# Graph network kernel: expansion ahead of the gathers, landed rows added by Vector, node numbers fetched 16 steps at a time

## The chip, the cores and the metric

The kernel runs on one core of one Trainium2 chip. The metric is the device time of one execution in microseconds, lower is better. It was measured three times before the change: 10926.67, 10941.0 and 10946.07 us, median 10941.0.

## The reference, cut to what matters

A graph has N = 12500 nodes with 64 channels and E = 200000 edges (`src`, `dst`, 16 attributes each), sorted by `dst`, whose distribution is uneven. Two blocks follow each other, each with a residual and a layer norm around it; each block goes over the edges twice.

```python
# block 1, two times (relu after each)
z = concat([x[dst], x[src]]); m = sigmoid(z @ Wf + bf) * softplus(z @ Ws + bs)
x = x + segment_sum(m, dst)
# block 2, two times (batch norm after each): attention over the edges and a self loop per node
alpha = leaky_relu(a_src[src] + a_dst[dst] + a_edge)
p = exp(alpha - segment_max(alpha)[dst]) / segment_sum(...)
out = segment_sum(xl[src] * p, dst)
```

## The kernel before, in words

Nodes lie in NB = 98 blocks of P = 128. Setup sorts the edges into steps: a step is up to 128 edges, one per partition, which all go to one block of 128 destination nodes. There are STEPS = 1664 steps in 13 batches of 128. Eight steps are a unit (UNIT; 208 units in a stage), and most buffers exist twice (SETS = 2), one for even units and one for odd ones. `dst_rel` holds each edge's node number within its block, and `rel_rows` in HBM the same by step, as bf16, for the transposed use.

The four edge stages are the loops over all steps. The first two (`cg_edges`, block 1) do this per unit. GpSimd issues a gather for each step (L706): 128 rows of 128 floats from `q_table`, the source node's part of z @ W, into `ring`, four groups of four steps. SyncE fetches the unit's node numbers to all 128 partitions (L684), one DMA per unit. Vector compares them with the partition's number and so makes the transposed one-hot (L737). TensorE forms `pre` in PSUM, in two halves of four steps (`form`): it adds the gathered rows by a matmul with the identity (L797), and expands the destination node's part out of `p_tab` with the transposed one-hot (L801). Scalar takes |pre|, Exp and Ln (L766 to L771), Vector finishes both softplus halves (L742, L743), Scalar does one more Exp (L776), Vector multiplies to the message (L749) and makes the one-hot (L587, in `build_onehot`). TensorE sums the messages by node (`segment_sum`, L815, between an opening and a closing matmul, L602 and L609), and Vector adds the eight sums to the accumulator (L728).

The last two stages (`gat_edges`, block 2) gather 65 floats per step (L1166) into two buffers of a whole batch each, expand two numbers per edge with the transposed one-hot (L1187, L1382), do the softmax of a batch while the messages of the batch before it are summed, and then weigh and sum as above (L1289, L587, L1434, L1284). Their node numbers are fetched by L1137, one DMA per unit.

Nothing plans the order; each engine runs its own list, written out by `stages(u, first, last, (lag, what), ...)`: in turn u it does `what` for unit u - lag, in the order of the list. In `cg_edges` Vector's turn is `add(u-3), spread(u-1), onehot_t(u), softs(u-1), message(u-1)`, and TensorE's is the first half of `form(u)`, the second half of the sums of u-2, the second half of `form(u)`, the first half of the sums of u-1. The engines meet at semaphores, and the ones that matter are these. GpSimd may gather into a group's slot when TensorE has formed the half that used it (`s_X0`, `s_X`, L697). TensorE's identity matmul waits for the gathered rows (`s_row`). Scalar and Vector wait for `s_X`; Vector's `add` for the closed sums (`s_agg`); the expansion for the one-hot (`s_T`). SyncE fetches into a slot when Vector has read it; there are four slots of a unit each in `cg_edges` and two in `gat_edges`. In `gat_edges` GpSimd gathers into a buffer's slots unit by unit, when Vector has made the messages of two batches before (`e_m`), and Vector's one-hot waits for the expansion before it (`a_X`).

Of the kernel before, what the change touches and what calls it, by code (L numbers as in the profile page):

```python
# [23 lines left out]
P = 128  # L24
# [626 lines left out]
def cg_edges(k, layer):  # L651
# [4 lines left out]
    (s_zero, s_S, s_T, s_X0, s_X, s_ln, s_softf, s_softs, s_sig, s_msg, s_agg, s_acc, s_idx, s_act) = (  # L656
        k.sem(n + x) for x in ("zero", "onehot", "onehot_t", "pre_half", "pre", "ln", "soft_f", "soft_s", "sig", "msg", "agg", "acc", "idx", "act"))
# [3 lines left out]
    s_rel = [k.sem(f"{n}rel{q}") for q in range(CG_UNROLL)]  # L661
    p_tab = k.big[:, 0:NB * 2 * C]
    ring = k.big[:, NB * 2 * C:NB * 2 * C + RING].rearrange("p (u i c) -> p u i c", u=UNROLL, c=2 * C)
    acc = k.wide[:, NB * C:NB * (C + AW)]
    rel = rel_slots(k.wide[:, 0:CG_UNROLL * GROUP * P], CG_UNROLL)
    at = CG_UNROLL * GROUP * P
    turned = by_set(k.wide[:, at:at + UNROLL * GROUP * P].rearrange("p (u i c) -> p u i c", u=UNROLL, c=P))
    soft = by_set(k.work[:, 0:UNROLL * GROUP * P].rearrange("p (u i c) -> p u i c", u=UNROLL, c=2 * C))
    onehot, msg = by_set(k.onehot), by_set(k.msg)
    pre = [k.pairs[j][:, :, :].rearrange("p u (i c) -> p (u i) c", c=2 * C) for j in range(SETS)]  # L670
# [4 lines left out]
    with nc.Block() as block:  # L675
        @block.sync
        def _(sp):
            k.clear_old(sp)

            def fetch(it):  # L680
                for q in range(CG_UNROLL):
                    wait(sp, s_T, (it - 1) * CG_UNROLL + q + 1 if not isinstance(it, int) or it else 0)
                    sp.sem_inc(s_turn, 1)
                    sp.dma_start(rel[q], rel_row(k, it * CG_UNROLL + q)).then_inc(s_rel[q], 16)  # L684
            fetch(0)
            with sp.Fori(1, CG_ITERS) as it:
# [27 lines left out]
        def _(v):  # L714
# [5 lines left out]
            def iteration(it, first, last):  # L720
                n = counts(v, it * CG_UNROLL, -3, 3)
# [12 lines left out]
                def onehot_t(c):  # L734
                    v.wait_ge(s_rel[c], it * 16 + 16)
                    wait(v, s_X, n[c - 1])
                    nc.vector.tensor_scalar(turned[c % SETS].rearrange("p i c -> p (i c)"), rel[c], k.iota_col[:, :], None, ALU.is_equal).then_inc(s_T, 1)  # L737
# [13 lines left out]
                for u in range(CG_UNROLL):  # L751
                    stages(u, first, last, (3, add), (1, spread), (0, onehot_t), (1, softs), (1, message))
# [30 lines left out]
        def _(pe):  # L783
            def iteration(it, first, last):
                n = counts(pe, it * CG_UNROLL, -2, 4)
                gathered = it * (CG_UNROLL // SETS * 16 * GROUP)
                blocks, slots = {}, {}

                def form(c, half):

                    j, u = c % SETS, 2 * (c % SETS) + half
                    if half == 0:
                        blocks[c] = load_offsets(k, pe, TAB_ROW, it * (CG_UNROLL * UNIT) + c * UNIT, UNIT, (NB - 1) * 2 * C)
                    pe.wait_ge(s_row[u], gathered + (16 * GROUP * (c // SETS + 1) + row_base[u]))
                    if half == 0:
                        wait(pe, s_softs, n[c - 1])
                    nc.tensor.matmul(k.psum[u][:, :], k.ident[:, :], ring[:, u].rearrange("p i c -> p (i c)"), start=True, stop=False)  # L797
# [827 lines left out]
```

## Time and profile before

| | |
|---|---|
| three runs | 10926.67, 10941.0, 10946.07 us |
| the profiled execution's own time | 10924.85 us |
| its span, first to last instruction | 10923.1 us |
| TensorE, GpSimd, Vector, Scalar busy | 56, 62, 35, 17% |
| mean granted TensorE clock | 0.612 of full |
| gathers | 2 x 3328 |
| fetches of node numbers | 832, 256 KB each |

How to read it: the profile is one execution. PE is TensorE's matmul part and PEld its weight loads, DVE is Vector, ACT Scalar, POOL GpSimd, SP SyncE. L12 is line 12 of the kernel above, and a line can be that of a helper. A busy time counts no register, branch or issue work. The end of a matmul is modelled. An fp32 matmul has two records. "Idle before" is the engine's idle time just before the group's instructions, with what ended it: "issue" is that nothing shown was waited for, "remote" that a semaphore was updated at a time at which no instruction shown had just ended.

### The profile page before, as it was taken

How to read it: one execution, taken by the hardware profiler on the slowest of the kernel's cores; microseconds unless marked ns; L12 is line 12 of the kernel's file. 1: busy time of each engine (PE TensorE's matmuls, PEld its weight loads, DVE VectorE, ACT ScalarE, POOL GpSimd, SP SyncE). 2: the span in 40 equal slices, each digit the busy share in tenths (PEclk: the TensorE clock that was granted, in tenths of full speed). 3: DMA queues.
4: the chain of work that ended last, by engine and by line, in shares of the span. 5: the costliest groups of instructions: out<-in, count | busy, mean ns of one | idle time of the engine just before them, and what ended most of it. 6: DMA issues, size and time to landing. Idle time of an engine off the chain costs nothing. (4 is left out here: it accounts for less than half of the span.)

```text
span 10923.1 us, 113136 instructions
## 1 busy us (share of the span) xinstructions
PE 6133.0 (56%) x30283; PEld 4722.4 (43%) x30284; DVE 3780.2 (35%) x5844; ACT 1828.7 (17%) x2603; POOL 6747.6 (62%) x6802
## 2 busy tenths in 40 slices
PE   2777777777777777777413444444471344444446
PEld 1555555555555555555303333333350333333335
DVE  6333333333333333333402323223250222332226
ACT  1333333333333333333200000000010000000000
POOL 2666666666566666666366666666606666666661
PEclk6777777777777777777555555555555555555555
DMA  4222222222222222222322212222112221222221
GB/s 138 65 65 66 67 66 66 67 66 63 77 65 66 65 66 67 66 66 66 69 49 43 45 42 45 44 44 45 39 21 48 44 45 42 43 44 45 43 43 26
DMA packets 436626, 612.01 MB, mean 56 GB/s; under 512 B 180134, under 2 KB 217754, under 8 KB 434779
## 3 DMA queue, kind: packets, MB, share of 16 engines
q0 software_dynamic: 214032, 332.71, 13.7%
q1 hardware_dynamic: 217116, 262.20, 8.3%
q10 hardware_dynamic: 5193, 13.44, 0.4%
q8 instruction: 162, 2.65, 0.1%
q14 instruction: 123, 1.01, 0.0%
HBM read 575.04 MB, written 32.78 MB: 56 GB/s over the span
## 5 line engine op out<-in xcount | busy, mean ns | idle before, releaser
L706 POOL DMA_INDIRECT big<-q_table,idx_stage x3328 | 3309.7, 995 | 1592.7 <-issue 957.9
L1166 POOL DMA_INDIRECT big<-xl_table,idx_stage x3328 | 3336.2, 1002 | 1524.1 <-issue 1018.9
L1434 PE MATMUL bank<-msg,onehot 128*128 128x66 f32 x6656 | 1603.1, 410 | 1025.8 <-issue 974.9
L1434 PEld LDWEIGHTS bank<-msg,onehot 128*128 128x128 f32 x6656 | 1510.3, 325 | 1196.2 <-issue 1194.7
L801 PEld LDWEIGHTS bank<-big,wide 128*128 128x128 f32 x6656 | 1243.0, 263 | 1451.8 <-issue 1450.4
L801 PE MATMUL bank<-big,wide 128*128 x6656 | 1289.8, 351 | 774.3 <-DVE wide L737 495.3
L797 PE MATMUL bank<-big,ident 128*128 128x512 f32 x1664 | 1261.6, 846 | 172.9 <-DMA big<-q_table,idx_stage 93.0
L815 PE MATMUL bank<-msg,onehot 128*128 128x67 f32 (+1 forms) x6656 | 1156.7, 324 | 313.2 <-issue 213.5
L815 PEld LDWEIGHTS bank<-msg,onehot 128*128 128x128 f32 x6656 | 1073.9, 241 | 450.7 <-issue 448.9
L1284 DVE TENSOR_TENSOR wide<-wide,bank 128x528 f32 x416 | 293.0, 704 | 2457.6 <-DMA work<-in_dst 896.8
L587 DVE TENSOR_TENSOR onehot<-iota,dst_rel 128x1024 f32<-128x1024 f32 x832 | 1014.9, 1220 | 0.0
L1382 PE MATMUL bank<-spread_bf,big 128*128 x3328 | 275.6, 172 | 1292.8 <-issue 1166.4
L766 ACT ACTIVATE work<-bank 128x1024 f32<-128x1024 f32 x416 | 424.6, 1021 | 3041.0 <-remote 2502.8
L728 DVE TENSOR_TENSOR wide<-wide,bank 128x536 f32 (+1 forms) x416 | 291.7, 701 | 1724.3 <-remote 1610.3
L1382 PEld LDWEIGHTS bank<-spread_bf,big 128*128 128x128 bf16 x3328 | 200.4, 105 | 1363.0 <-issue 1347.3
L742 DVE SCALAR_TENSOR_TENSOR work<-bank,work 128x512 f32<-128x512 f32 x416 | 287.6, 691 | 1356.8 <-issue 698.9
L602 PE MATMUL bank<-zero_bf 1*128 1x268 bf16 x1664 | 467.6, 365 | 439.2 <-DVE onehot_t L1199 222.3
L1187 DVE TENSOR_SCALAR big<-big,iota_col 128x1024 bf16<-128x1024 bf16 x416 | 207.1, 500 | 1064.3 <-remote 911.0
L771 ACT ACTIVATE work<-work 128x1024 f32<-128x1024 f32 x416 | 439.6, 1057 | 51.6
L768 ACT ACTIVATE work<-work 128x1024 f32<-128x1024 f32 x416 | 439.6, 1057 | 13.3
L797 PEld LDWEIGHTS bank<-big,ident 128*128 128x128 f32 x1664 | 325.1, 241 | 220.8 <-issue 112.0
L1355 ACT ACTIVATE msg<-work 128x16 f32<-128x16 f32 x224 | 48.4, 220 | 2052.8 <-DMA work<-in_dst 648.4
(226 smaller groups left out, 3515.3 us busy)
## 6 DMA issues: line engine op xcount, KB each, us to landing
wide<-rel_rows SPq DMA_DIRECT2D x416, 256.0 KB
big<-rel_rows SPq DMA_DIRECT2D x416, 256.0 KB
big<-q_table,idx_stage POOLq DMA_INDIRECT x3328
big<-xl_table,idx_stage POOLq DMA_INDIRECT x3328
q_table<-wide SPq DMA_DIRECT2D x12, 1024.0 KB, 5.1
edge_rows<-big SPq DMA_DIRECT2D x25, 257.0 KB, 6.4
xl_table<-big SPq DMA_DIRECT2D x12, 520.0 KB, 6.6
big<-in_edge_attr ACTq DMA_DIRECT2D x6, 1024.0 KB
```

What stands on the lines that cost most here:

```text
L587: return nc.vector.tensor_tensor(to, k.iota[:, :].unsqueeze(1).broadcast_to([P, UNIT, P]), k.dst_rel[:, ds(s, UNIT)].unsqueeze(2).broadcas ...
L602: nc.tensor.matmul(pair[:, half, :].rearrange("p (i c) -> p i c", c=P)[:, :, 0:AW], k.zero_bf[:, :], k.zero_bf[:, 0:AW].unsqueeze(1).broad ...
L706: pool.indirect_dma_start(out=ring[:, group % UNROLL, s % GROUP, :], out_offset=None, in_=k.q_table, in_offset=bass.IndirectOffsetOnAxis(a ...
L766: nc.scalar.activation(soft[j], pre[j], ACT.Abs).then_inc(s_act, 1)
L768: nc.scalar.activation(soft[j], soft[j], ACT.Exp, scale=-1.0).then_inc(s_act, 1)
L771: nc.scalar.activation(soft[j], soft[j], ACT.Ln, bias=1.0).then_inc(s_ln, 1)
L797: nc.tensor.matmul(k.psum[u][:, :], k.ident[:, :], ring[:, u].rearrange("p i c -> p (i c)"), start=True, stop=False)
L801: last_one = nc.tensor.matmul(k.psum[u][:, i * P:(i + 1) * P], turned[j][:, half * GROUP + i, :], p_tab[:, ds(blocks[c][half * GROUP + i], ...
L815: nc.tensor.matmul(agg[j][:, ds(slots[i], width)], onehot[j][:, s, :], msg[j][:, s, 0:width], start=False, stop=False)
L1166: pool.indirect_dma_start(out=buf[p][:, s, :], out_offset=None, in_=k.xl_table, in_offset=bass.IndirectOffsetOnAxis(ap=k.idx_stage[:, s:s ...
L1382: last_one = nc.tensor.matmul(near[:, ds(column + (c * UNIT + i) * SLOT, 2 * PARTS)], turned[c % SETS][:, i, :], spread_bf[:, ds(at[i], 2 ...
L1434: nc.tensor.matmul(sums_of[j][:, ds(slots[i], C + 2)], onehot[j][:, i, :], msg[j][:, i, 0:C + 2], start=False, stop=False)
```

## The change

Of `rel_slots`, `rel_row` and the new `rel_unit`: a slot now holds the numbers of two units, and one DMA of 512 KB fills it. All four edge stages have two such slots. In `cg_edges` the identity matmul goes. `form` expands eight steps at once into `near` (PSUM), with start=True, and waits for no gathered row. A new operation `land` of Vector waits for the unit's rows and adds them: `pre = near + landed`, where `pre` is now in SBUF (`wide`). Scalar and the softplus operations read it there and wait for the new semaphore `s_Z`. GpSimd waits for `s_Z` once per unit. The lags change: Vector's turn is `add(u-4), onehot_t(u), land(u-1), spread(u-2), softs(u-2), message(u-2)`, TensorE's is `form(u)` and then all eight sums of u-3.

```diff
-def rel_slots(words, count):
-    return [words[:, q * GROUP * P:(q + 1) * GROUP * P].bitcast(BF16) for q in range(count)]
-def rel_row(k, unit):
-    return k.rel_rows.rearrange("(q s) e -> q (s e)", s=UNIT)[ds(unit, 1), :].broadcast_to([P, UNIT * P])
+def rel_slots(words):
+    return [words[:, q * UNIT * P:(q + 1) * UNIT * P].bitcast(BF16) for q in range(2)]
+def rel_row(k, pair):
+    return k.rel_rows.rearrange("(q s) e -> q (s e)", s=2 * UNIT)[ds(pair, 1), :].broadcast_to([P, 2 * UNIT * P])
+def rel_unit(slot, unit):
+    return slot[:, unit * UNIT * P:(unit + 1) * UNIT * P]
...
@@ cg_edges, SyncE
-                for q in range(CG_UNROLL):
-                    wait(sp, s_T, (it - 1) * CG_UNROLL + q + 1 if not isinstance(it, int) or it else 0)
+                for q in range(2):
+                    wait(sp, s_T, (it - 1) * CG_UNROLL + 2 * q + 2 if not isinstance(it, int) or it else 0)
                     sp.sem_inc(s_turn, 1)
-                    sp.dma_start(rel[q], rel_row(k, it * CG_UNROLL + q)).then_inc(s_rel[q], 16)
+                    sp.dma_start(rel[q], rel_row(k, it * 2 + q)).then_inc(s_rel[q], 16)
@@ cg_edges, GpSimd
-                    if s % GROUP == 0:
-                        wait(pool, (s_X0, s_X)[group % 2], b * BUNITS + ((group - UNROLL) // 2 + 1))
+                    if s % UNIT == 0:
+                        wait(pool, s_Z, b * BUNITS + (s // UNIT - 1))
@@ cg_edges, Vector
+                def land(c):
+                    j = c % SETS
+                    for half in range(2):
+                        u = 2 * j + half
+                        v.wait_ge(s_row[u], gathered + (16 * GROUP * (c // SETS + 1) + row_base[u]))
+                    wait(v, s_X, n[c + 1])
+                    nc.vector.tensor_tensor(pre[j], near[j], landed[:, j], ALU.add).then_inc(s_Z, 1)
...
-                    stages(u, first, last, (3, add), (1, spread), (0, onehot_t), (1, softs), (1, message))
+                    stages(u, first, last, (4, add), (0, onehot_t), (1, land), (2, spread), (2, softs), (2, message))
@@ cg_edges, Scalar
-                    wait(act, s_X, n[c + 1])
+                    wait(act, s_Z, n[c + 1])
@@ cg_edges, TensorE
-                    nc.tensor.matmul(k.psum[u][:, :], k.ident[:, :], ring[:, u].rearrange("p i c -> p (i c)"), start=True, stop=False)
...
+                def form(c):
+                    j = c % SETS
+                    blocks = load_offsets(k, pe, TAB_ROW, it * (CG_UNROLL * UNIT) + c * UNIT, UNIT, (NB - 1) * 2 * C)
+                    wait(pe, s_Z, n[c - 1])
+                    wait(pe, s_T, n[c + 1])
+                    for i in range(UNIT):
+                        last_one = nc.tensor.matmul(near[j][:, i, :], turned[j][:, i, :],
+                                                    p_tab[:, ds(blocks[i], 2 * C)], start=True, stop=True)
+                    last_one.then_inc(s_X, 1)
...
-                    stages(u, first, last, (0, lambda c: form(c, 0)), (2, lambda c: segment_sum(c, 1)),
-                           (0, lambda c: form(c, 1)), (1, lambda c: segment_sum(c, 0)))
+                    stages(u, first, last, (0, form), (3, segment_sum))
@@ gat_edges, SyncE
-                for q in range(GAT_UNROLL):
-                    wait(sp, a_T, (it - 1) * GAT_UNROLL + q + 1 if not isinstance(it, int) or it else 0)
+                for q in range(2):
+                    wait(sp, a_T, (it - 1) * 2 * GAT_UNROLL + (q + 1) * GAT_UNROLL if not isinstance(it, int) or it else 0)
                     sp.sem_inc(s_turn, 1)
-                    sp.dma_start(rel_pair[q], rel_row(k, it * GAT_UNROLL + q)).then_inc(s_rel[q], 16)
+                    sp.dma_start(rel[q], rel_row(k, it * 2 + q)).then_inc(s_rel[q], 16)
```

## Rows read from the trace of the kernel before

**Rows 1.** The page, engines' busy time and share.

```profile
PE 6133.0 (56%) x30283; PEld 4722.4 (43%) x30284; DVE 3780.2 (35%) x5844; ACT 1828.7 (17%) x2603; POOL 6747.6 (62%) x6802
```

**Rows 2.** Stages: us, busy of PE, PEld, DVE, ACT, POOL; clock, DMA share, GB/s.

```profile
256.80:2735.00 2478.20, 1825.53 (x8232) 1335.26 (x8233) 929.08 (x1238) 795.25 (x1031) 1661.02 (x1690) 0.72 0.23 66
2803.00:5284.20 2481.20, 1801.49 (x8241) 1321.39 (x8242) 924.52 (x1236) 773.23 (x825) 1662.74 (x1690) 0.74 0.24 66
5408.80:7901.00 2492.20, 986.48 (x5359) 821.51 (x5359) 662.43 (x1241) 53.00 (x224) 1680.36 (x1690) 0.50 0.21 45
8162.50:10673.50 2511.00, 991.64 (x5389) 824.40 (x5390) 667.63 (x1250) 53.60 (x227) 1680.34 (x1690) 0.50 0.21 44
```

**Rows 3.** The page, gathers: out<-in xcount | busy us, mean ns | idle before.

```profile
L706 POOL DMA_INDIRECT big<-q_table,idx_stage x3328 | 3309.7, 995 | 1592.7 <-issue 957.9
L1166 POOL DMA_INDIRECT big<-xl_table,idx_stage x3328 | 3336.2, 1002 | 1524.1 <-issue 1018.9
```

**Rows 4.** Timeline of a convolution stage: start, us, engine, line [idle before].

```profile
2036.92 1.05 PE L801 MATMUL bank<-big,wide 128*128 x8
...
2040.76 1.22 DVE L587 TENSOR_TENSOR onehot<-iota,dst_rel 128x1024 f32<-128x1024 f32 x1
2041.52 1.27 POOL L706 DMA_INDIRECT big<-q_table,idx_stage  x1 [0.30 <-issue]
...
2042.89 0.64 SPq L684 DMA_DIRECT2D wide<-rel_rows  x1
...
2045.59 0.95 POOL L706 DMA_INDIRECT big<-q_table,idx_stage  x1 [0.30 <-issue]
...
2048.62 1.02 ACT L766 ACTIVATE work<-bank 128x1024 f32<-128x1024 f32 x1 [12.93 <-remote]
...
2049.29 0.94 POOL L706 DMA_INDIRECT big<-q_table,idx_stage  x1 [2.75 <-remote]
```

**Rows 5.** GpSimd's waits: for whom, us, times, longest.

```profile
POOL big L706 <- remote: 622.7, 249, 4.3
POOL big L1166 <- DVE msg L1289: 438.8, 63, 13.4
...
POOL big L706 <- PE bank L801: 10.5, 23, 3.8
```

**Rows 6.** Timeline of an attention stage, TensorE and then GpSimd.

```profile
6994.23 0.37 PE L1394 MATMUL bank<-ident,work 128*128 128x128 f32 x1 [2.63 <-issue]
6997.73 0.37 PE L1394 MATMUL bank<-ident,work 128*128 128x128 f32 x1 [3.13 <-issue]
...
7008.94 1.33 PE L1434 MATMUL bank<-msg,onehot 128*128 128x66 f32 x5 [0.23 <-issue]
...
7002.17 0.94 POOL L1166 DMA_INDIRECT big<-xl_table,idx_stage  x1 [0.30 <-issue]
```

**Rows 7.** Waits put down to remote.

```profile
ACT work L766 <- remote: 2502.8, 231, 20.1
DVE wide L728 <- remote: 1610.3, 246, 17.8
...
DVE big L1187 <- remote: 911.0, 90, 22.0
```

**Rows 8.** The page, operations of the convolution stages, and L1434.

```profile
L1434 PE MATMUL bank<-msg,onehot 128*128 128x66 f32 x6656 | 1603.1, 410 | 1025.8 <-issue 974.9
...
L797 PE MATMUL bank<-big,ident 128*128 128x512 f32 x1664 | 1261.6, 846 | 172.9 <-DMA big<-q_table,idx_stage 93.0
L815 PE MATMUL bank<-msg,onehot 128*128 128x67 f32 (+1 forms) x6656 | 1156.7, 324 | 313.2 <-issue 213.5
...
L742 DVE SCALAR_TENSOR_TENSOR work<-bank,work 128x512 f32<-128x512 f32 x416 | 287.6, 691 | 1356.8 <-issue 698.9
```

**Rows 9.** The page, fetches of node numbers.

```profile
wide<-rel_rows SPq DMA_DIRECT2D x416, 256.0 KB
big<-rel_rows SPq DMA_DIRECT2D x416, 256.0 KB
```

More of the change, by code:

```diff
@@ L784, in iteration @@
             def iteration(it, first, last):
[L785 to L796, printed above, removed]
-                    nc.tensor.matmul(k.psum[u][:, :], k.ident[:, :], ring[:, u].rearrange("p i c -> p (i c)"), start=True, stop=False)
-                    if half == 0:
-                        wait(pe, s_T, n[c + 1])
-                    for i in range(GROUP):
-                        last_one = nc.tensor.matmul(k.psum[u][:, i * P:(i + 1) * P], turned[j][:, half * GROUP + i, :],
-                                                    p_tab[:, ds(blocks[c][half * GROUP + i], 2 * C)], start=False, stop=i == GROUP - 1)
-                    last_one.then_inc((s_X0, s_X)[half], 1)
@@ L805, in segment_sum @@
-                def segment_sum(c, half):
-                    j = c % SETS
-                    if half == 0:
-                        wait(pe, s_acc, n[c])
-                        open_span(nc, k, k.pairs[SETS + j])
-                        wait(pe, s_msg, n[c + 1])
-                        wait(pe, s_S, n[c + 1])
-                    slots = load_offsets(k, pe, SPAN_ROW, it * (CG_UNROLL * UNIT) + c * UNIT + half * GROUP, GROUP, (UNIT - 1) * P)
-                    for i in range(GROUP):
-                        s = half * GROUP + i
-                        nc.tensor.matmul(agg[j][:, ds(slots[i], width)], onehot[j][:, s, :],
-                                                    msg[j][:, s, 0:width], start=False, stop=False)
-                    if half:
-                        close_span(nc, k, k.pairs[SETS + j]).then_inc(s_agg, 1)
+                n = counts(pe, it * CG_UNROLL, -3, 4)
@@ new lines, in segment_sum @@
+                def segment_sum(c):
+                    j = c % SETS
+                    slots = load_offsets(k, pe, SPAN_ROW, it * (CG_UNROLL * UNIT) + c * UNIT, UNIT, (UNIT - 1) * P)
+                    wait(pe, s_acc, n[c])
+                    open_span(nc, k, k.pairs[SETS + j])
+                    wait(pe, s_msg, n[c + 1])
+                    wait(pe, s_S, n[c + 1])
+                    for i in range(UNIT):
+                        nc.tensor.matmul(agg[j][:, ds(slots[i], width)], onehot[j][:, i, :],
+                                         msg[j][:, i, 0:width], start=False, stop=False)
+                    close_span(nc, k, k.pairs[SETS + j]).then_inc(s_agg, 1)
@@ L1065, in gat_edges @@
     s_turn = k.sem(n + "turn")
-    s_rel = [k.sem(f"{n}rel{q}") for q in range(GAT_UNROLL)]
+    s_rel = [k.sem(f"{n}rel{q}") for q in range(2)]
     acc = k.wide[:, NB * C:NB * (C + AW)]
@@ L1182, in _, with turn_onehot, turn_first @@
             v.wait_ge(s_zero, 2)
[L1184 to L1185 removed]
+            def turn_onehot(c, slot, pair, n):
+                v.wait_ge(s_rel[slot], pair * 16 + 16)
                 wait(v, a_X, n[c - 1])
[L1187 to L1193 removed]
+                nc.vector.tensor_scalar(turned[c].rearrange("p i c -> p (i c)"), rel_unit(rel[slot], c), k.iota_col[:, :], None, ALU.is_equal).then_inc(a_T, 1)
+            def turn_first(pair):
+                for slot in range(2):
+                    n = counts(v, pair * 2 * GAT_UNROLL + slot * GAT_UNROLL, -1, 0)
+                    for c in range(GAT_UNROLL):
+                        turn_onehot(c, slot, pair, n)
+            turn_first(0)
+            with v.Fori(1, BIT // 2) as pair:
+                turn_first(pair)
             def near_copy(b, link):
@@ L1298, in sums @@
                         if spreads(b):
-                            stages(u, first, last, (0, lambda c: turn_onehot(c, (b + 2) * BIT + it, ahead)))
+                            stages(u, first, last, (0, lambda c: turn_onehot(c, it % 2, (b + 2) * (BIT // 2) + it // 2, ahead)))
                 if not begins(b):
```

37 lines of the change are left out of this document (17 added, 20 removed).

## The prediction, made blind

> **What bounds the kernel now.** I read the page first, then a table of the four edge stages, then GpSimd's waits, then two short timelines. The page gives TensorE 56% and GpSimd 62% busy [rows 1]: no engine is full. The four edge stages last 2478.2, 2481.2, 2492.2 and 2511.0 us, 9962.6 of 10923.1 us [rows 2], so all else is about 960 us and the change doesn't touch it. One unit (8 steps) takes 2478.2/208 = 11.91 us in the convolution stages and 2501.6/208 = 12.03 in the attention stages.
>
> The steadiest work in all four is GpSimd's gathers, one per step: 995 and 1002 ns each, and 0.30 us between two even when nothing is waited for [rows 3, 4]. That makes 8 x (0.995 + 0.305) = 10.40 us per unit, the floor of this kernel as long as each step has its own gather. What lies above it is GpSimd's idle time beyond 0.305 us per gather: 1592.7 - 1015 = 578 us in the convolution stages and 1524.1 - 1015 = 509 in the attention stages. In the former nearly all of it is waiting for TensorE's signal that a ring slot was read (622.7 us in 249 waits, the releaser is given as remote, and 10.5 in 23, both with the 0.3 in them), 272 waits of 2.33 us; in the latter it is waiting for Vector's messages (438.8 us in 63 waits) [rows 5]. At most 578 + 509 = 1087 us can be won.
>
> Why does GpSimd wait for a TensorE that is 73% busy there? The timeline shows that the cause is less its load than when its signals arrive. The last expansion of a unit is recorded at 2036.92 to 2037.97, yet Scalar, which waits for it and for nothing later, starts at 2048.62. In between GpSimd issues gather on gather until 2046.54 and pauses for want of a free slot; two microseconds into that pause TensorE moves again, Scalar starts, and at 2049.29 the gathers go on [rows 4]. A fetch of node numbers had been issued at 2042.89. In the attention stage the same is longer: TensorE starts single matmuls at 6994.23 and 6997.73, waiting for nothing shown; GpSimd's last gather before a pause ends at 7003.11, and TensorE is back at 0.2 us per matmul at 7008.94 [rows 6]. Scalar's 2502.8 us and Vector's 1610.3 and 911.0 us of waits with releaser remote are this [rows 7]. I read it so: after a fetch TensorE can fall into a slow, held state, and mostly leaves it when GpSimd pauses. The pauses are then part of the cycle, and their number and length decide the time. That the fetch is the trigger is the weakest link; rows 4 and 6 allow it, they don't prove it.
>
> **The change part by part.**
>
> *Identity matmul out, Vector's addition in (convolution stages).* TensorE loses 1664 records, 1261.6 us busy, of about 3600 [rows 2, 8]: 3.0 us per unit. It is not on GpSimd's floor, so by itself it saves nothing; it shortens what follows a release. The two stages run at a granted clock of 0.72 and 0.74 of full, a mix of 1.2 and 2.4 GHz; the attention stages, where TensorE is 40% busy, are at 0.50, all 1.2 GHz [rows 2]. With less work the convolution stages may fall there: a matmul record then costs 410 instead of 324 ns [rows 8]. Records overlap: five in a row take 1.33 us there [rows 6], so (1.33 - 0.41)/4 = 0.23 us each. A unit has 8 expansions and 8 sums of two records, 32 x 0.23 = 7.4 us, still under 10.4. Vector gains one addition of 128x1024 from PSUM and SBUF; not in the trace, bounded by L742 (512 columns of PSUM and SBUF, 691 ns) below and twice that, 1.38 us, above; I take 1.2, as L587 does 1024 columns in 1.22 [rows 4]. Vector is busy 929.1/208 = 4.5 us per unit [rows 2] and comes to 5.7 of 12: hidden, except that it now lies between TensorE's signal and the freeing of a slot.
>
> *Order of the work.* Expansion no longer waits for gathered rows but for Vector having consumed the bank two units before. Its signal is due about a unit earlier than now. Gathers of unit m wait for the addition of unit m-2, once per 8 steps instead of per 4: the same ring of 16 steps, coarser. If Vector sits in the addition waiting for rows, behind it are the one-hot (1.22), the two softplus operations (0.69 each) and the message of the previous unit (512 columns too, so 0.7), 3.3 us, then the next transposed one-hot, which TensorE waits for. With 10.4 us per unit and 5.7 of work that is covered in a smooth run; after a held stretch it is not.
>
> *Softplus from SBUF.* L742 and L743 read PSUM and SBUF now and will read SBUF twice. The trace shows that a gather beginning while Vector runs an operation on two SBUF inputs is stretched: the one of 2041.52 begins under L587 (until 2041.98) and lasts 1.27 instead of 0.94, to 0.81 us after Vector's end [rows 4]. Two operations of 0.69 us, with gathers every 1.25 us: a start falls in the harmful 0.56 us in 45% of the cases and costs 0.28 on average, 0.13 us for each, 0.25 per unit, 105 us over 416 units. Taken as one stretch of 1.3 us it is 0.55 per unit, 230 us; below, nothing, where GpSimd waits anyway. I take 80. The Trainium skill (SBUF — State Buffer, section "Who interferes with whom") states it as a rule: a Vector instruction with two SBUF inputs contends with a GpSimd instruction that reads SBUF, one with at most one SBUF input doesn't. By that rule the new addition is free and the softplus pays; the stretched gather agrees, and without the rule the sum would be 80 us better.
>
> *Fetches of 16 steps.* 832 fetches of 256 KB [rows 9] become 416 of 512 KB, same bytes, all from SyncE's queue. The slots hold four units in all, as before in the convolution stages and instead of two in the attention stages, and a slot is fetched again when both its units are read, so two units (over 20 us) before it is needed: I cost the landing at nothing. Were it late, Vector's one-hot and with it the expansion would be, which B's price covers. What counts is how often TensorE gets into the held state: half as often if each fetch may trigger it, the same if bytes do.
>
> **The sum (forecast).** Convolution stages: the 272 waits halve to 136, but each now holds the addition too, 2.33 - 0.30 + 1.2 = 3.2 us: 435 us instead of 578, less 143; plus 80 for contention: 63 saved. Attention stages: nothing moves but the fetches; 509 us of waits halve: 255 saved. Together 318. The profiled execution took 10924.85 us, 1.8 beyond its span and 16 below the median of 10941.0; 10925 - 318 = 10607, and 16 more for a median: 10620.
>
> **Rivals.**
>
> *A, GpSimd at its floor in the convolution stages.* The expansion has a unit more of slack and TensorE a third less work, so its signals always arrive before the ring is full. 578 - 80 = 498 saved, with 255 in attention 753: 10941 - 753 = 10190. For it: Vector has 10.4 - 5.7 = 4.7 us to spare per unit, TensorE 10.4 - 7.4 = 3.0 even at its lower clock. Against it: attention stages have even more slack (two batches) and TensorE 40% busy, and still wait 509 us.
>
> *B, slower: the release chain lengthens.* The held state follows bytes or the gathers themselves, not the number of fetches. Then 272 pauses stay, and in each the slot is freed only after TensorE's signal, Vector's waiting accumulation, its transposed one-hot (about 0.7 each, by L742) and the addition (1.2): 2.03 + 2.6 = 4.63 us, 1259 us instead of 578, and 80 for contention, nothing in attention: 761 slower at worst; with the addition alone in the chain 3.2 us, 870 us, 372 slower, which I take as its time since the other two are mostly done by then: 11310. It decides once a pause costs over 578/272 = 2.1 us at an unchanged count. For it: pauses follow the full ring, which is as small as before and freed in coarser pieces.
>
> *C, the fetches don't matter, and the convolution part evens out.* Attention unchanged, convolution within 60 us either way: 10900.
>
> **How the numbers follow.** Forecast 0.40, A 0.20, B 0.27, C 0.13, the last two by how little the trace says of the trigger. A measurement of this kernel can tell about 0.2% from no change, 22 us. C splits in three nearly equal parts, and the forecast's own spread (10450 to 10800) stays faster but for 0.02. Faster: 0.38 + 0.20 + 0.05 = 0.63; same 0.06; slower 0.27 + 0.04 = 0.31. The range runs from A (10190, with 40 us for its spread) to B's own time, of which half lies above: 10150 to 11300, leaving out some 0.18; the forecast's own is 10450 to 10800.
>
> **What would show it.** L797 gone and one addition of near 1.2 us with 416 entries in Vector's groups; if it is 1.4 or more, the price of a release was too low. GpSimd's waits in the convolution stages near 136, 3.5 us each: this is the forecast; near none is A, near 270 of 3.5 or more is B. Mean gather 995 ns rising to about 1020 shows the contention; unchanged means that it was nothing. In attention, GpSimd's waits for messages near half, and TensorE's idle time before L1434 (974.9 us put down to issue, [rows 8]) near half too; if these stay, the fetches were not the trigger. Granted clock in the convolution stages: 0.50 if the lighter TensorE lost the upper level. What makes the prediction wrong above all: a held state with another cause.

## The result, and the profile after

The changed kernel is slower: 11206.2 us median of 4 runs (11201.6 to 11212.8) against 10943.5 of before, ratio 1.0242, 95% interval 1.0228 to 1.0255. The forecast was 10620, faster; the loss is on rival B's side, at about 0.7 of its price.

The four stages and the groups that answer to [rows 2, 3, 8]:

```profile
266.70:2877.90 2611.20, 1533.87 (x7422) 1373.43 (x7422) 1158.18 (x1445) 806.40 (x1034) 1734.63 (x1690) 0.55 0.22 63
2943.60:5551.40 2607.80, 1529.12 (x7438) 1370.67 (x7438) 1154.24 (x1444) 763.67 (x828) 1740.25 (x1690) 0.55 0.22 63
5672.80:8171.20 2498.40, 973.34 (x5366) 813.38 (x5366) 660.58 (x1241) 53.09 (x226) 1683.27 (x1690) 0.50 0.21 45
8431.00:10938.40 2507.40, 980.34 (x5366) 817.38 (x5366) 663.20 (x1241) 53.36 (x226) 1683.03 (x1690) 0.50 0.21 44
```
```profile
L715 POOL DMA_INDIRECT big<-q_table,idx_stage x3328 | 3447.3, 1036 | 1713.2 <-issue 1005.8 <-DVE wide L755 705.8 <-POOL idx_stage L717 1.6
L1172 POOL DMA_INDIRECT big<-xl_table,idx_stage x3328 | 3344.0, 1005 | 1521.7 <-issue 1043.9 <-DVE msg L1298 413.1 <-remote 63.1
...
L755 DVE TENSOR_TENSOR wide<-bank,big 128x1024 f32<-128x1024 f32 x416 | 504.5, 1213 | 61.2 <-remote 24.4 <-DMA big<-q_table,idx_stage 22.3 <-issue 14.5
```

The attention stages kept their time (5005.8 us against 5003.2), GpSimd's idle time there (1521.7 against 1524.1) and TensorE's before L1443, the L1434 of before (974.1, of it 882.2 put down to issue, against 1025.8 and 974.9). The two convolution stages took 5219.0 us instead of 4959.4: 259.6 of the span's 276.4. That is 137.6 us in gathers (3447.3 - 3309.7; 1036 ns each instead of 995) and 120.5 us in GpSimd's idle time (1713.2 - 1592.7). TensorE's granted clock fell from 0.72 and 0.74 to 0.55, nearly all at 1.2 GHz.

A break is from here on a stretch of over 1 us between two gathers of the convolution stages. There were 260 of 2.71 us on average before and 165 of 4.82 after (705 and 795 us in all). A timeline of one shows what is in it (start, us, engine, line, idle before):

```profile
1059.35 0.20 PE L609 MATMUL bank<-zero_bf 1*128 1x1 bf16 x2
...
1067.60 0.95 POOL L715 DMA_INDIRECT big<-q_table,idx_stage  x1 [0.30 <-issue]
1071.33 0.22 ACT L792 ACTIVATE msg<-ae 128x16 f32 x1 [11.62 <-remote]
1071.34 0.71 DVE L738 TENSOR_TENSOR wide<-wide,bank 128x536 f32 x1 [14.11 <-remote]
1071.97 0.75 DVE L747 TENSOR_SCALAR wide<-wide,iota_col 128x1024 f32<-128x1024 bf16 x1
1072.63 1.22 DVE L755 TENSOR_TENSOR wide<-bank,big 128x1024 f32<-128x1024 f32 x1
...
1073.77 1.22 DVE L587 TENSOR_TENSOR onehot<-iota,dst_rel 128x1024 f32<-128x1024 f32 x1
1074.80 1.00 POOL L715 DMA_INDIRECT big<-q_table,idx_stage  x1 [6.25 <-DVE wide L755]
```

L609 closes the sums at 1059.55, and its signal is all that L792 and L738 wait for, yet both start at 1071.33: it came 11.8 us late. GpSimd gathers through all of that, runs out of slots at 1068.55, and the signal comes 2.8 us later. Then accumulation, transposed one-hot and landing addition run one after another and the gathers resume. In 121 of the 165 breaks Vector runs those two after the last gather and ahead of the addition, and on average these breaks take 5.70 us: TensorE's first signal comes 2.05 us after the last gather, the addition starts 1.60 later and takes 1.22, and the next gather starts 0.83 after it. In 31 breaks the addition has all of that behind it when the last gather ends, and mostly runs already; these take 2.10 us. Before, the first signal came after 1.98 us and freed the slot directly. So the held TensorE of the prediction (its signals come late while GpSimd gathers) is there in both kernels, also where its matmuls are recorded evenly.

### The profile page after: what moved, and what is told of

Read it like the earlier page. It is cut to its first block and busy times, and to the rows that moved or that the text cites. A ratio compares the mean times of both kernels' runs of the same rounds, so it can differ in the third digit from the quotient of the medians.

```text
span 11199.5 us, 107118 instructions
## 1 busy us (share of the span) xinstructions
PE 5543.6 (49%) x28619; PEld 4796.2 (43%) x28620; DVE 4238.5 (38%) x6260; ACT 1823.8 (16%) x2603; POOL 6930.9 (62%) x6802
## 5 line engine op out<-in xcount | busy, mean ns | idle before, releaser
L715 POOL DMA_INDIRECT big<-q_table,idx_stage x3328 | 3447.3, 1036 | 1713.2 <-issue 1005.8
L1172 POOL DMA_INDIRECT big<-xl_table,idx_stage x3328 | 3344.0, 1005 | 1521.7 <-issue 1043.9
L811 PE MATMUL bank<-big,wide 128*128 x6656 | 1542.5, 425 | 2159.5 <-DVE wide L747 1835.6
L811 PEld LDWEIGHTS bank<-big,wide 128*128 128x128 f32 x6656 | 1431.5, 327 | 2194.0 <-issue 2194.0
L1443 PE MATMUL bank<-msg,onehot 128*128 128x66 f32 x6656 | 1589.5, 412 | 974.1 <-issue 882.2
L1443 PEld LDWEIGHTS bank<-msg,onehot 128*128 128x128 f32 x6656 | 1502.5, 325 | 1173.2 <-issue 1172.8
L738 DVE TENSOR_TENSOR wide<-wide,bank 128x536 f32 (+1 forms) x416 | 291.7, 701 | 2812.5 <-remote 2000.2
L823 PE MATMUL bank<-msg,onehot 128*128 128x67 f32 (+1 forms) x6656 | 1306.9, 377 | 15.4 <-issue 10.4
L823 PEld LDWEIGHTS bank<-msg,onehot 128*128 128x128 f32 x6656 | 1233.9, 286 | 177.1 <-issue 177.1
L587 DVE TENSOR_TENSOR onehot<-iota,dst_rel 128x1024 f32<-128x1024 f32 x832 | 1011.3, 1216 | 0.0
L602 PE MATMUL bank<-zero_bf 1*128 1x268 bf16 x1664 | 505.7, 397 | 414.3 <-issue 228.8
L794 ACT ACTIVATE work<-work 128x512 f32<-128x512 f32 x416 | 262.2, 630 | 2666.3 <-DVE work L760 2494.9
L755 DVE TENSOR_TENSOR wide<-bank,big 128x1024 f32<-128x1024 f32 x416 | 504.5, 1213 | 61.2 <-remote 24.4
L784 ACT ACTIVATE work<-wide 128x1024 f32<-128x1024 f32 x416 | 432.9, 1041 | 29.3 <-issue 14.9
L602 PEld LDWEIGHTS bank<-zero_bf 1*128 1x128 bf16 x1664 | 111.0, 105 | 547.5 <-issue 519.9
```

The source lines that it names most:

```text
L587: return nc.vector.tensor_tensor(to, k.iota[:, :].unsqueeze(1).broadcast_to([P, UNIT, P]), k.dst_rel[:, ds(s, UNIT)].unsqueeze(2).broadcas ...
L602: nc.tensor.matmul(pair[:, half, :].rearrange("p (i c) -> p i c", c=P)[:, :, 0:AW], k.zero_bf[:, :], k.zero_bf[:, 0:AW].unsqueeze(1).broad ...
L715: pool.indirect_dma_start(out=ring[:, group % UNROLL, s % GROUP, :], out_offset=None, in_=k.q_table, in_offset=bass.IndirectOffsetOnAxis(a ...
L755: nc.vector.tensor_tensor(pre[j], near[j], landed[:, j], ALU.add).then_inc(s_Z, 1)
L784: nc.scalar.activation(soft[j], pre[j], ACT.Abs).then_inc(s_act, 1)
L811: last_one = nc.tensor.matmul(near[j][:, i, :], turned[j][:, i, :], p_tab[:, ds(blocks[i], 2 * C)], start=True, stop=True)
```

## The experiments

Ratios are against the kernel before on the same chip, with 95% intervals. The sets ran on different chips, and these differ: the kernel before took 11054 and 11082 us on two of them, and 9650 to 9657 us on three others. On the former TensorE is held as above, on the latter it isn't.

**Vector's order.** Theory first held: Vector's accumulation ahead of the one-hot makes a serial loop.

```
(4, add), (0, onehot_t), (1, land), (2, spread), (2, softs), (2, message)      the changed kernel
(0, onehot_t), (1, land), (4, add), (2, spread), (2, softs), (2, message)      e1a
(0, onehot_t), (1, land), (2, softs), (4, add), (2, spread), (2, message)      e1b
```

> Theory L (serial loop): in the changed kernel Vector's accumulation of unit u-4 stands ahead of the transposed one-hot of unit u and waits for all sums of TensorE's round before, so each unit costs a round of TensorE plus Vector's accumulation, one-hot and two signals. Here the one-hot and the landing addition stand ahead of the accumulation; nothing else changes. L expects a unit of 11.0 to 11.4 us instead of 12.55, GpSimd's idle time beyond 0.305 us per gather in the two convolution stages down from 705 to under 350 us, and in all 10570 to 10730 us. Rival R (coarse release): the ring is freed in steps of 8 rows after a signal of TensorE and an addition, whatever Vector does before; then 11150 to 11250 us, idle time unchanged.

> As the kernel above, but the softplus operations too stand ahead of the accumulation (one-hot_t, landing addition, softplus, accumulation, one-hot, message). L: as above or up to 50 us less, since Scalar's last step starts earlier: 10520 to 10730 us. R: 11150 to 11250. Contention (gathers stretched under Vector's operations on two SBUF inputs): landing addition and softplus stand back to back here and the gathers' mean stays at 1036 ns or rises; where the accumulation lies between the landing addition and the one-hot (the kernel above) it falls to 1010 to 1025 ns if the run of operations back to back is what stretches them.

Measured 11353.9 us, 1.0264 (1.0239 to 1.0289), and 11224.2 us, 1.0141 (1.0122 to 1.0160). The theory fell: breaks 144 of 6.55 us and 119 of 6.29, fewer and longer. Sorted by what Vector does between the last gather and the addition, they come in two kinds. In e1a 88 have nothing ahead of the addition and take 4.27 us; in 53 the accumulation of the turn before, which itself waits for a late signal, and the five operations behind it stand ahead of the addition, which then starts 8.38 us after the last gather, and the break takes 10.41 us. In e1b it is 75 of 4.81 and 40 of 9.10. In these the accumulation, moved behind one addition, stands with all that follows it ahead of the next. The gathers took 1030 and 1043 ns, where 1010 to 1025 and 1036 or more were expected.

TensorE's hold shows here in its own records too, its matmuls and weight loads starting 0.70 us or a multiple of that apart (e1a, TensorE):

```profile
964.08 0.37 PE L811 MATMUL bank<-big,wide 128*128 x1 [1.03 <-issue]
964.81 0.55 PE L811 MATMUL bank<-big,wide 128*128 x1 [0.36 <-issue]
967.63 0.37 PE L811 MATMUL bank<-big,wide 128*128 x1 [2.27 <-issue]
```

e1b, at 1.0141, lies below the changed kernel (1.0242, and 1.0280 on another chip; it wasn't run on this one) and is still behind the kernel before.

**Fetches alone, pipeline alone.** e2 is the kernel before with the 16-step fetches in all edge stages, e3 the changed kernel with 8-step fetches in its convolution stages.

> The kernel before with the fetches of 16 steps alone (all four edge stages). Theory: fetches don't matter, since the attention stages, where they are the whole change, kept their time: 10920 to 10960 us, idle time of GpSimd in the convolution stages near 580 us. Rival F (the reading of the prediction, fewer fetches give fewer pauses in the convolution stages, and the rest of the change hid it): idle time there down by a quarter or more, 10650 to 10800 us. Rival G: larger fetches cost by themselves: over 11000 us.

> The changed kernel with the fetches of 8 steps put back in the convolution stages, so the rearranged pipeline alone there. Theory: 11190 to 11220 us. Rival F: more fetches, more pauses: 11350 us or more. Rival G: under 11100 us.

e2 11022.5 us, 0.9960 (0.9945 to 0.9974); e3 11381.9, 1.0287 (1.0270 to 1.0305). GpSimd's waits in the convolution stages of e2:

```profile
POOL big L711 <- remote: 680.5, 260, 4.4
```

About as many pauses as in [rows 5] (249). e3's time lies where its rival F put it, but the chip is slower too: by ratio e3 is the changed kernel (1.0280 in a1 below), with 186 breaks of 5.32 us beside a1's 173 of 5.37. The fetches are not the trigger; the loss is the pipeline's.

**Who holds TensorE.** p3: in the first convolution stage SyncE copies rows instead of gathers; in the second the gathers are halved. q3: the first as in p3, the second as it is.

```
 for x in range(GROUP):
     sp.dma_start(ring[:, u, x, :], k.q_table[x * P:(x + 1) * P, :]).then_inc(s_row[u], 16)
```

> The kernel before. First convolution stage: no gathers; SyncE copies 128 rows in order from the table into the ring for each step (as many bytes and rows, wrong rows). Second: the gathers fetch half of each row (256 bytes instead of 512). Attention as before. If GpSimd's gathers are what holds TensorE, the first stage has no held TensorE and its unit is bound by SyncE's issue or Vector's chain, under 10 us. If the traffic of the rows does it, the holds stay in the first stage and go or thin out in the second. If neither (a matter of TensorE alone), both stages keep them.

> The kernel before; first convolution stage without gathers (SyncE copies 128 rows in order for each step, wrong rows), second convolution stage as it is. On a chip with the held state: if the gathers hold TensorE, matmuls 0.70 us apart are in the second stage and in the attention stages and not in the first, whose unit stays under 8 us (6.5 us on the chip without holds, where it took 1394 us for 208 units and some start-up). If the hold has nothing to do with GpSimd, the first stage has as many microseconds of it per unit as the second.

p3 met a chip on which the kernel before takes 9656 us: 8783.9 us, 0.9096 (0.9070 to 0.9123); nothing is held there in any stage. q3 met a slow kind: 9879.6 us, 0.8918 (0.8897 to 0.8938). Its two convolution stages:

```profile
265.00:1646.00 1381.00, 1324.49 (x8761) 1017.07 (x8759) 946.99 (x1278) 833.62 (x1083) 0.00 (x0) 0.99 0.43 122
1650.00:4165.60 2515.60, 1835.35 (x8242) 1350.62 (x8242) 925.45 (x1237) 774.70 (x826) 1667.20 (x1690) 0.72 0.25 65
```

Without gathers 6.6 us per unit, TensorE busy 96% at 2.4 GHz and twice the bytes per second (122 against 65 GB/s). Each signal paired with the record that gives it, 3 in 626 of TensorE's came over 1.5 us after the record's start; with gathers 342 in 539 (in p3's second stage, on the other chip, 0 in 611). So it is the gathers that hold TensorE, not its own load and not the bytes, and only on some chips. What it is in them, GpSimd's work, its queue or the scattered rows, no run separates.

**TensorE's load and GpSimd's pace.** p4 is the changed kernel with single-record matmuls (the expansions in the first convolution stage, the sums too in the second), p1 the kernel before with memsets between gathers.

```
 high(turned[j])[:, i, :], high(p_tab)[:, ds(blocks[i], 2 * C)]          p4, expansions (upper 16 bits)
 if layer == 0 or s % UNIT == UNIT - 1:                                  p1
     nc.gpsimd.memset(spare[:, 0:1024 if layer else 1], 0.0).then_inc(s_pad, 1)
```

> The changed kernel with fewer TensorE records: in the first convolution stage the expansions take the upper 16 bits of their operands (one record for each matmul instead of two; the values are rounded), in the second the sums too. Theory: in a held stretch TensorE gets through one record per 0.70 us, and what it has not done by the end of the stretch lengthens GpSimd's pause; with 16 of 36 records fewer the idle time beyond 0.305 us per gather of the first stage falls from 350 to about 200 us, with both (32 of 68 left as 20) under 150 in the second: 12.55 us per unit become 11.8 and 11.4. Rival (the pause is the chain of Vector's operations after the release, whatever TensorE has left): both stages within 0.2 us of 12.55.

> The kernel before, with GpSimd slowed: in the first convolution stage a memset of one column (near 0.12 us) after every gather, in the second a memset of 1024 columns (about 1.05 us) after every 8 gathers; the attention stages as before. Theory H: an unbroken run of gathers brings TensorE into a held state (its matmuls then start 0.70 us or a multiple apart, or its signals come up to 12 us late); it hardly ever begins in the first 10 us after a pause and ends 2 to 5 us after the last gather. If pauses clear it, the one of 1 us per unit in the second stage shortens or thins it out: the waits of 0.7 us and more fall from 121 to under 80 there, and the stage takes 11.5 to 12.0 us per unit instead of 11.93 in spite of 1.05 us more work of GpSimd. Theory S (TensorE's hold has nothing to do with the gathers' breaks): both stages get longer, or TensorE's waits are swallowed by the slack: between 11.9 and 13.0 us per unit with as many holds.

On the chip without holds: p4 9635.9 us, 0.9982 (0.9970 to 0.9993); p1 9894.3, 1.0246 (1.0217 to 1.0276), 10.82 and 11.53 us per unit.

> The changed kernel with one TensorE record per matmul instead of two, in the first convolution stage for the expansions, in the second for the sums too (rounded values). The set before got a chip without held TensorE, so the question stands. With the held state: what TensorE has left to do when it is released lengthens the pause, so the first stage takes 11.8 and the second 11.4 us per unit instead of 12.55. Rival, the pause is Vector's chain alone: both within 0.2 of 12.55.

> The kernel before with a memset of one column after each gather (first convolution stage) and one of 1024 columns, 1.05 us, after every 8 gathers (second). On a chip with the held state: if breaks of 1 us clear or delay the hold, the second stage has fewer than 80 pauses of 0.7 us beyond the memset's own and takes 11.5 to 12.0 us per unit; if not, 12.3 to 13.0 with 100 pauses or more. Without the held state: 10.82 and 11.53 us, as measured in the last set.

With holds: p4 11306.8 us, 1.0206 (1.0182 to 1.0230). Its two convolution stages:

```profile
259.10:2990.40 2731.30, 1153.61 (x5754) 937.29 (x5755) 1148.61 (x1445) 798.22 (x1032) 1661.85 (x1690) 0.50 0.21 60
3056.90:5625.70 2568.80, 557.92 (x4126) 347.20 (x4126) 1152.74 (x1444) 762.59 (x827) 1713.94 (x1690) 0.50 0.22 64
```

13.13 and 12.35 us per unit, beside 12.84 and 12.82 of the changed kernel there: the first stage got slower, the second won less than half of what was expected. The theory fails, and so does the rival in the first stage, where it allowed 0.2 us; TensorE busy 22% still leaves 61 breaks of 6.3 us. p1 11091.2 us, 1.0007 (0.9995 to 1.0018): 12.20 and 12.02 us per unit, beside 12.09 of q3's unaltered stage. The second stage's memsets, 970 ns each and some 200 us in all, cost about that much where TensorE isn't held. Where it is, they cost nothing: the pauses beyond the memset's own fell to 73, as p1's theory had it (under 80), from 129 of that length in q3's stage, and what they saved is what the memsets took.

**The changed kernel again.**

> The changed kernel, unaltered, on whatever chip this set gets. On a chip where TensorE is held as in the first traces: 1.018 to 1.030 of the kernel before, pauses of 4 to 6 us in the convolution stages, attention near 12.0 us per unit. On a chip without the held state (the last set had one: the kernel before took 9656 us there, attention 10.53 us per unit) GpSimd's gathers bound all four stages; then 0.995 to 1.006, no pauses over 0.7 us, and a gather of 1010 to 1030 ns.

On q3's chip 11380.8 us, 1.0280 (1.0259 to 1.0302), as expected, 173 breaks of 5.37 us, gathers 1032 ns. The breaks sort as in the first trace: 146 with accumulation and transposed one-hot ahead of the addition take 5.95 us (signal after 2.16), 18 with nothing ahead 1.85. The kernel was not run on a chip without holds.

**What stretches the gathers.** p2 is the kernel before with softplus on two SBUF inputs (first convolution stage) or an unused landing addition (second).

```
 scalar_tensor_tensor(soft[j][:, :, f_half], read[j][:, :, f_half], ...)   read = spare if layer == 0 else pre
 if layer: nc.vector.tensor_tensor(spare[j], pre[j], other[j], ALU.add)
```

> The kernel before with one piece of the change at a time as dead work, off the chain of releases. First convolution stage: the two softplus operations read a buffer in SBUF instead of PSUM (the values aren't those of the expansion). Second: an addition of 1024 columns, PSUM and SBUF into SBUF, between the two softplus operations, result unused. If the longer gathers of the changed kernel (995 to 1036 ns) come from the softplus on two SBUF inputs, the gathers of the first stage rise to 1015 to 1040 ns and those of the second stay at 995. If they come from the addition, it is the other way round. If neither alone does it, they come from operations standing back to back without a break: both stay under 1010.

> The kernel before with single pieces of the change as in the second set (first convolution stage: softplus on two SBUF inputs; second: an unused addition of 1024 columns, PSUM and SBUF into SBUF, between the two softplus operations). Without held TensorE the gathers took 1028 and 1014 ns beside 1010 to 1012 in attention. With it, and 995 ns as the level of the kernel before: if the softplus is the cause of the changed kernel's 1036 ns, the first stage shows 1010 to 1030 and 12.2 us per unit or more; the second 995 to 1000 ns and 12.0 to 12.3 us.

Twice on chips without holds: 9663.8 us, 1.0010 (0.9999 to 1.0022), and 9665.0, 1.0009 (0.9999 to 1.0018). The gathers of the second run, first and second stage:

```profile
L709 POOL DMA_INDIRECT big<-q_table,idx_stage x1664 | 1720.2, 1034 | 504.1 <-issue 483.5 <-PE bank L808 19.8 <-POOL idx_stage L711 0.8
...
L709 POOL DMA_INDIRECT big<-q_table,idx_stage x1664 | 1679.5, 1009 | 504.1 <-issue 479.9 <-PE bank L808 23.5 <-POOL idx_stage L711 0.8
```

1034 and 1009 ns (1028 and 1014 in the first run). Sorted by the operation of Vector under which a gather starts, the reason is plain: in the first stage the 209 gathers that start under the softplus took 1141 ns on average, 41 us in all over the usual 947 ns; in the second the 204 under the same two operations, there on PSUM and SBUF, and the 202 under the added addition took 946 ns. The Trainium skill (SBUF — State Buffer, section "Who interferes with whom") has this as a rule: a Vector instruction with two SBUF inputs contends with a GpSimd instruction that reads SBUF, and one with at most one SBUF input doesn't, outside the modes in which Vector uses both of its port pairs. The two stages agree with it. The whole kernel took only 8 us more than the kernel before (1.0009), though, so most of the 41 were saved under other operations; there is no trace of the kernel before on such a chip to say where.

In the changed kernel the same sorting puts the stretch elsewhere: 242 us of it on the 392 gathers that start under the one-hot L587 (1564 ns on average), where the kernel before has 130 us on 292 (1390 ns); under the softplus 6 us. A gather that starts under L587 ends 0.82 us after L587's end. This is how the costliest of them come to start there:

```profile
1207.65 0.86 DVE L747 TENSOR_SCALAR wide<-wide,iota_col 128x1024 f32<-128x1024 bf16 x1
1208.31 1.02 POOL L715 DMA_INDIRECT big<-q_table,idx_stage  x1 [0.30 <-issue]
...
1209.56 1.21 DVE L587 TENSOR_TENSOR onehot<-iota,dst_rel 128x1024 f32<-128x1024 f32 x1
1209.63 1.97 POOL L715 DMA_INDIRECT big<-q_table,idx_stage  x1 [0.30 <-issue]
```

The transposed one-hot L747 has one SBUF input and holds a gather too, until 0.81 us after its end (202 of the 210 that start under it); by the rule it would have to be in one of the modes excepted, which no run here shows. The next gather starts 0.30 us later, and the landing addition in between is just long enough for L587 to have started 0.07 us before: the gather waits out the whole of it. 182 gathers start like this one, within 0.1 us of L587's start; they took 1962 ns, 185 us over the usual, and 180 of them follow a gather held by L747. a1 has 174 of them (174 us). The gathers that end a break are not the reason: 146 of these start under L587, but mostly 0.86 us into it or later, and lose 29 us.

**The release.** b1 is the kernel before, ring freed once per unit, in the first stage through an operation of Vector; b3 has fetches of 16 steps and the release once per unit; b4 is the changed kernel with the landing in halves.

```
 if s % UNIT == 0:
     wait(pool, s_X if layer else s_read, b * BUNITS + (s // UNIT - 1))                      b1; b3: s_X
 nc.vector.tensor_tensor(pre[j][:, own], near[j][:, own], landed[:, j, own], ALU.add)        b4, twice
```

> The kernel before, with the release of the ring changed alone. Second convolution stage: GpSimd waits once per 8 steps for TensorE's signal of the whole unit two before (coarse release, nothing of Vector in it). First: the same, but through Vector, by an operation of 1024 columns with one SBUF input (it reads the landed rows; its result isn't used) that waits for TensorE's signal. Theory (the chain of the release): on a chip with the held state the coarse release alone gives 75 to 95 pauses in the stage instead of 125, of 2.7 to 3.3 us, 11.6 to 12.0 us per unit; through Vector each pause is 1.0 to 2.0 us longer, 12.2 to 12.7 us per unit. Rival (the rest of the change, order and TensorE's clock, makes the pauses long): both stages within 0.15 of 12.1. Without the held state: both at 10.5 to 10.7.

> The kernel before with the fetches of 16 steps in all edge stages and the coarse release by TensorE's signal in both convolution stages; TensorE's identity matmul and softplus from PSUM stay. Theory: fewer pauses of unchanged length, 0.975 to 0.992 of the kernel before. Rival: the coarser release loses what it gains (a slot comes free later), 0.995 to 1.010.

> The changed kernel, its landing addition split in two of 512 columns with a signal each, for which GpSimd waits every 4 steps. Theory: GpSimd goes on after the first half, so a pause is 0.5 to 0.7 us shorter (4.2 instead of 4.8), but there are more of them; 0.990 to 1.000 of the changed kernel, 1.010 to 1.025 of the kernel before. Rival (pause ends with what TensorE catches up, not with the chain): the pauses keep their 4.8 us.

> The kernel before with the release of the ring changed alone (first convolution stage: once per 8 steps, through an operation of Vector that waits for TensorE's signal; second: once per 8 steps by TensorE's signal itself). The set before got a chip without held TensorE: 10.68 and 10.63 us per unit, no pauses. On a chip with it the theory of the release chain expects 75 to 95 pauses of 2.7 to 3.3 us and 11.6 to 12.0 us per unit in the second stage, and pauses 1.0 to 2.0 us longer, 12.2 to 12.7 us per unit, in the first. Rival (order of Vector's work and TensorE's clock make the pauses long): both within 0.15 of 12.1.

> The kernel before with fetches of 16 steps and the coarse release by TensorE's signal. Without held TensorE it took 0.994 of the kernel before. With it: theory (fewer pauses of the same length) 0.975 to 0.992; rival (slots come free later) 0.995 to 1.010.

Both sets met chips without holds, so the question of the pauses wasn't answered. There b1 took 9674.6 and 9672.8 us, 1.0022 (1.0012 to 1.0032) and 1.0023 (1.0013 to 1.0034), 10.68 and 10.72 us per unit through Vector, 10.63 and 10.55 without; b3 9592.9 and 9576.7, 0.9937 (0.9925 to 0.9948) and 0.9923 (0.9907 to 0.9940); b4 9603.4, 0.9944 (0.9930 to 0.9958). Idle time was the plain 0.303 us per gather in all of these, so within the four stages they differ by the gathers' duration alone. The gathers of b4:

```profile
L715 POOL DMA_INDIRECT big<-q_table,idx_stage x3328 | 3341.8, 1004 | 1007.8 <-issue 963.5 <-DVE wide L757 42.7 <-POOL idx_stage L717 1.6
```

b4 has the changed kernel's operations and 1004 ns. In it 174 gathers follow one held by the transposed one-hot, as above, and none of them is stretched: Vector waits for the rows of the landing then, and the one-hot comes later. The same holds for p4 on the chip without holds (210, none stretched). How the gathers fall against Vector's operations counts as much as which these are.

## Why the prediction was wrong

**What failed first** is the step that the prediction called its weakest link: "after a fetch TensorE can fall into a slow, held state", so fewer fetches, fewer holds. In the attention stages, where the fetches are the whole change, GpSimd's idle time was 1521.7 us against 1524.1; the 255 us credited there were 2. The prediction took it from one fetch that lay near one held stretch. e2 and e3 say the same of the convolution stages. q3 shows the gathers in the place of the fetches.

**The count and the length of pauses.** 272 of 2.33 us were to become 136 of 3.2, 143 us less. By one bound (1 us) they went from 260 of 2.71 to 165 of 4.82, 90 us more, and with the shorter ones 120 more. The count fell as with a coarser release, to 0.63 instead of 0.5; why not further is open. The length was mis-sized: 1.2 us were added for the addition, and 2.1 came. The rest is accumulation and transposed one-hot, queued ahead of the addition when the late signals arrive; the prediction named them in B ("about 0.7 each") and left them out "since the other two are mostly done by then". They mostly weren't: in 121 of 165 breaks both were still to run, and 1.60 us passed between the signal and the addition. TensorE's part of such a break is what it was (2.05 us to its first signal, 1.98 before), so its lower clock doesn't show in it. a1 repeats both findings. In e1a the list was changed, and where it was longer (six operations), it took 4.5 us instead of 1.60 and the break 10.41. So that list adds its own duration to a break wherever the signal is late; the experiment that changed the release alone, b1, met no held TensorE.

**Rival B** was right in sign and mechanism (a slot is freed only after TensorE's signal and Vector's operations) and wrong in its count (272 stay); its 372 us are 96 above the 276 of the profiled executions. **A** did not come here; 10.5 to 10.6 us per unit, which is near it, is what the changed kernel's relatives b4 and p4 show on chips without holds. **C** was half right: attention unchanged.

**Contention**: 80 us taken, between 0 and 230; 137.6 measured, inside the bounds by luck. The term was put on the softplus, on the assumption that a gather starts under it by chance in 45% of the cases. Only 20 gathers started under its first operation, and 371 under its second, all in its last 0.1 us and none of them stretched, since the gather before (in 370 of the 371) had been held by the one-hot. The softplus took 6 us in all. Instead the one-hot took 112 us more than before, the transposed one-hot 22 (28 instead of 6), the accumulation 9, and the message 20 less; and the undisturbed gather, 947 ns instead of 944, another 10. The prediction gave the rule without the modes that it excepts, and so had no term for an operation with one SBUF input.

**The addition's duration** was right (1.2 taken, 1213 ns, 416 entries). **The clock** fell as allowed for, to 0.55; what that alone costs the whole kernel no run isolates.

**Accounting.** Forecast: -143 pauses, +80 contention, -255 attention, -318 in all. Measured: +120, +138, +3, and some 14 outside the four stages.

**Best version.** No kernel was faster on both kinds of chip. On chips with holds e2 (the fetches alone) is the only one under the kernel before, 0.9960. On those without, b3 is at 0.9937 and 0.9923, b4 at 0.9944, and p4, with its rounded values, at 0.9982; how b3 and b4 do with holds stays open. None of these differences reaches 1%.

## What to carry to other kernels

When two engines wait for each other through a third, count what is queued in front of the releasing operation at the moment the late signal comes, not in a smooth run. Before a stall is credited to a trigger, look in the profile for a stage in which the change touches nothing but that trigger. Where one engine's operation holds up another's, look also at what the next one then starts under: the order of the operations can cost more than the new operation. And when an engine's waits can't be explained from its own rows, find out whether they come with the chip: an edit that costs 2.5% on one (p1) cost nothing on another.

## What the runs showed of the hardware

- The same kernel took 10943.5, 11053.9 and 11081.6 us in three sets and 9655.7, 9656.6 and 9650.3 in three others, on other chips. Nine tenths of the difference lie in the edge stages: 9962.6 us in the trace of the kernel before, 8809.6 in that of p2, whose whole time is within 0.1% of the kernel before on its chip. On the chips without holds GpSimd idles 0.303 us per gather and no more; with them it is 0.48 and 0.46 in the trace of the kernel before. What sets the chips apart wasn't found.
- The hold: signals 12 us late and more, or matmuls 0.70 us or a multiple apart. It is rare at first after a break (in the changed kernel 12 of the 133 expansions that started in the first 5 us had a late signal, later 101 of 238). TensorE's first signal comes about 2 us after the last gather in the convolution stages (3.2 in e1a); in the attention stages its matmuls run evenly again about 4 us after it (median of 92 breaks before, 81 after).
- A matmul's recorded end doesn't date its signal: L609 ended at 1059.55 and its semaphore moved at 1071.21.
- A gather that starts under the one-hot, 1.22 us with two SBUF inputs, ends 0.82 us after it (388 of 392 in the changed kernel) and took up to 1.99 us instead of 0.94; of the 415 that start under the softplus on PSUM and SBUF in the kernel before, none was stretched (944 ns).
- Under the transposed one-hot, with one SBUF input, gathers were stretched too: 202 of 210 in the changed kernel, 159 of 162 under b1's added operation in its second run; and 48 of 206 under the accumulation (L738), which runs just ahead of the transposed one-hot.
